# Eight query tiles regrouped over three attention rounds of a two-layer adaLN transformer kernel

## The reference, cut to what matters

```python
# h = layernorm(x) * (1 + ca) + sa              [4, 1024, 256]
latent_kv = h @ w_kv_down                       # rank 128
k, v = split(latent_kv @ w_kv_up)               # 16 heads of 64 each
q = h @ w_q                                     # 16 heads of 64
att = einsum('bqhd,bkhd->bhqk', q, k) * 64**-0.5
att = softmax(where(causal, att, -inf), axis=-1)
y = einsum('bhqk,bkhd->bqhd', att, v).reshape(B, T, 1024)
x = x + ga * (y @ w_out)
```

## Time and profile before

| What | Value |
|---|---|
| median of 3 runs | 1795.16 us |
| profiled execution, its span | 1797.59 us, 1796.3 us |
| TensorE busy | 1737.0 us, 97% |
| VectorE busy | 1250.7 us, 70% |
| ScalarE busy | 887.7 us, 49% |
| GpSimd busy | 854.0 us, 48% |
| granted TensorE clock, mean | 0.999 of full |
| one pair in the steady part of the attention (second batch) | 25.07 us |

### The profile page before, as it was taken

One profiled execution on the slowest core, in us unless ns is written; L12 is line 12 of the kernel. 1 busy time (PEld: TensorE's weight loads), 2 busy tenths in 40 slices (PEclk: granted clock), 3 DMA queues, 4 the chain that ended last, 5 costly groups with the idle time before them and its releaser, 6 DMA issues.

```text
span 1796.3 us, 40559 instructions
## 1 busy us (share of the span) xinstructions
PE 1737.0 (97%) x16006; PEld 1207.7 (67%) x16006; DVE 1250.7 (70%) x2766; ACT 887.7 (49%) x1968; POOL 854.0 (48%) x1282
## 2 busy tenths in 40 slices
PE   9999999999999999999999999999999999999998
PEld 5666685668566767566856667756685666766667
DVE  5888848626788885753678887675468888676545
ACT  4676634223577763322457775432246767443233
POOL 2777842221187874241138777314114877731410
PEclk9999999999999999999999999999999999999999
DMA  6555570321255554040135555305013555530500
GB/s 185 129 134 127 125 208 31 54 42 37 69 138 128 128 120 149 1 81 15 37 92 131 130 126 122 133 2 95 0 43 103 134 126 124 132 109 2 94 1 25
DMA packets 119915, 164.42 MB, mean 92 GB/s; under 512 B 30032, under 2 KB 86832, under 8 KB 118704
## 3 DMA queue, kind: packets, MB, share of 16 engines
q1 hardware_dynamic: 105760, 155.03, 35.9%
q10 hardware_dynamic: 13968, 6.82, 1.3%
HBM read 63.16 MB, written 4.24 MB: 38 GB/s over the span
## 4 chain that ended last, share of the span: by engine, by line
PE 72%; DVE 14%; ACT 5%; SPq 4%; DMA 3%; issue 1%; POOL 1%; ACTq 0%; DVEq 0%; POOLq 0%
PE scores L466 13%; PE bank L684 10%; PE scores L664 9%; PE bank L719 4%; PE bank L466 4%; SPq L1002 4%; DVE prob L813 3%; ACT prob L924 2%; PE scores L1776 2%; PE scores L1686 2%; PE scores L1114 2%; DMA placed<-prob 2%; PE bank L725 2%; PE bank L721 2%; PE scores L1748 2%; PE scores L437 2%
## 5 line engine op out<-in xcount | busy, mean ns | idle before, releaser
L882 POOL COPY placed<-prob 32x768 f32<-32x768 f32 x384 | 315.5, 822 | 27.5
L297 POOL TENSOR_TENSOR rstd<-rstd,minus_half 128x2 f32<-128x2 f32 x96 | 69.7, 728 | 533.1 <-DVE rstd L296 531.0
L684 PEld LDWEIGHTS bank<-placed,v_t 128*64 128x64 f32 x4608 | 250.0, 137 | 75.7 <-issue 70.5
L684 PE MATMUL bank<-placed,v_t 128*64 128x128 f32 x4608 | 272.7, 275 | 9.9 <-DMA placed<-hx 4.8
L664 PE MATMUL scores<-k_t,q_t 64*128 64x512 f32 (+3 forms) x1536 | 275.1, 496 | 0.8 <-ACT rec_t L934 0.8
L806 DVE CUSTOM_DVE_ANT_0 mod_rows<-scores,hx 128x128 f32<-128x128 f32 (+7 forms) x256 | 191.8, 749 | 75.5 <-PE scores L664 75.5
L813 DVE STREAM_TRANSPOSE prob<-prob 128x1536 f32<-128x1536 f32 x128 | 222.9, 1765 | 27.4 <-ACT prob L924 27.1
L806 DVE CUSTOM_DVE_ANT_0 x<-scores,hx 128x128 f32<-128x128 f32 (+7 forms) x256 | 192.7, 753 | 0.0
L924 ACT ACTIVATE prob<-mod_rows,neg_max 128x128 f32<-128x128 f32 (+2 forms) x192 | 137.3, 715 | 102.9 <-DVE neg_max L806 86.6
L664 PEld LDWEIGHTS scores<-k_t,q_t 64*128 64x128 f32 x1536 | 129.5, 186 | 85.1 <-issue 62.0
L870 POOL COPY rec_wide<-rec 128x128 f32<-128x128 f32 x256 | 65.0, 289 | 226.6 <-DVE rec L817 168.6
(11 more groups left out here) (249 smaller groups left out, 3435.8 us busy)
## 6 DMA issues: line engine op xcount, KB each, us to landing
placed<-prob SPq DMA_DIRECT2D x640, 96.0 KB, 2.2
f<-in_L_ffn_f SPq DMA_DIRECT2D x16, 2048.0 KB, 13.6
placed<-hx SPq DMA_DIRECT2D x320, 96.0 KB, 2.2
mod_rows<-mod_scratch SPq DMA_DIRECT2D x32, 128.0 KB, 4.3
out<-x SPq DMA_DIRECT2D x16, 256.0 KB, 2.2
w_ring<-in_L_attn_w_q ACTq DMA_DIRECT2D x24, 128.0 KB, 2.6
w_ring<-in_L_attn_w_kv_up ACTq DMA_DIRECT2D x48, 64.0 KB, 2.0
next_x<-in_L_attn_x SPq DMA_DIRECT2D x6, 512.0 KB, 4.1
```

The costliest lines, as they stand in the source:

```text
L297: step = pool.do(lambda e, ts=ts: nc.gpsimd.tensor_tensor(rstd[:, ts], rstd[:, ts], minus_half[:, ts], op=ALU.pow), var, filled)
L684: last = nc.tensor.matmul(out_bank[rows_, at_:at_ + P], v_t[pair % 2][:, j, rows_], placed[m % 2][:, :, head, first_block(m, i) + j, :], s ...
L882: nc.gpsimd.tensor_copy(placed[m % 2][target * GROUP:(target + 1) * GROUP, source, :, :, :], prob[m % 3][source * GROUP:(source + 1) * GRO ...
```

## The change

Which tiles share a round, and in which order they are worked on, changes. No instruction is of another shape, and there are as many of each shape as before. A round still has 12 blocks. A has the tiles 3, 5, 1 (6 parts), B has 7, 2, 0 (6 parts), C has 4, 6 as before (4 parts). `out_parts` follows: the three tiles 1, 3, 5 of A are evenly spaced and are copied and normalised by one instruction in place of two. Those of B (0, 2, 7) need two in place of one.

```diff
-        ROUND_TILES = ((0, 2, 1, 5), (3, 7), (4, 6))
+        ROUND_TILES = ((3, 5, 1), (7, 2, 0), (4, 6))
@@
         def out_parts(m):
-            return [(0, 2)] if len(tiles_in(m)) == 2 else [(0, 3), (3, 4)]
+            return [(0, 2), (2, 3)] if 7 in tiles_in(m) else [(0, len(tiles_in(m)))]
```

## The result

The changed kernel took 1847.57 us in the median of 4 runs (1846.05 to 1851.0), the kernel before 1794.65 us (4 runs, one more than in the table above). The ratio is 1.0297, with a 95% interval of 1.0279 to 1.0315: slower by 53 us. The profiled execution has a span of 1846.2 us, 49.9 more than before; the one of the kernel before was 2.9 us above its median, so what follows accounts for 50 of the 53. In the experiments the kernel before was timed again beside each group of runs, with medians of 1795.1 to 1795.5 us, so times of different sections can be compared to within about 1 us.

A forecast was written before the change was run, and what follows sets the result against it. TensorE's own order was taken to bound the steady rounds. B's waits 27.4, moves 8.8 and first rounds 13.2 gave +49.4 on 1797.6, 1847.0 profiled; with the median 2.4 lower, 1845 was forecast, range 1822 to 1868.

The forecast's parts named there:

- TensorE bound, nothing removed: Steady rounds: TensorE's own order sets the time; the change removes none of its work, nought in sum.
- The wait before k1: Each steady round B with projections: k1 waits 1.14 us for ScalarE's copy, bounds 0.9 to 1.4; 27.4 us in all.
- The steps 2.03, 3.30, 7.19, 7.60: Round B, us after scores begin: first minimum starts, its exponential starts, five exponentials end, copy ends and k1 starts.
- The wait for k1 covers the late shuffles: Rounds B and C: shuffles end later, but C's minima start just on time, so the two delays are not added.
- The moves of B: SyncE's ten DMAs after B's shuffles: values wait longer in 24 rounds, 7 x 0.77 + 17 x 0.2 = 8.8 us; bounds 0, 31.
- Rounds 0 to 3: First rounds, VectorE and ScalarE chain: +0.6 in round 0, +1.9 in 1, +0.8 in 3; 3.3 per batch, 13.2 us together.
- Tail: Last pair and output projections: nothing waits for the late copy and the projections keep their order; nought.
- The rival with slow moves: Moves of B at their upper bound, every last move taking 4.1 us: +72 us, 1867; chance 0.15.
- The rival by which the copy is not in the way: Round B: k1's wait is met earlier; only first rounds and some moves stay, +13 to +22, about 1812; chance 0.10.
- the one by which small last parts let the shuffles start sooner: Rounds A and B: small last part saves 0.76 us each, move waits go, first rounds shorten by 9; 1783; chance 0.04.
- "same" and "faster": Whole kernel's outcome: same, within 0.2% or 3.6 us, chance 0.04; faster, chance 0.05; slower had 0.91.
- no change: Rival for the whole kernel: everything hides behind TensorE, added exponentials use only slack; 1795; chance 0.05.

## Why the prediction was right, and where it was off

1845 was forecast, 1847.6 measured. The mechanism in the steady rounds is the one described, step for step; two terms of the sum were mis-sized, in opposite directions.

- **TensorE bound, nothing removed**: held. Counts are equal, and the kernel with the largest tile last takes the time of before.
- **The wait before k1**: forecast 1.14 us in each of 24 rounds, measured 1.05. The steps 2.03, 3.30, 7.19, 7.60 came out as 2.02, 3.37, 7.23 (the start of the copy) and 7.73; the semaphore's 0.04 was 0.15. k1 was due at 6.46 by the forecast and at 6.68 (7.73 - 1.05) in the trace. When TensorE has to stop in the middle of the block, the two pieces of L721 take 1.12 + 1.10 us in place of 1.98, 0.24 more. This term was missing. With it and the transposes (B one fewer, C one more) B and C together lost 1.29 us per pair, 31.0 in all, not 27.4. The 0.24 us, 24 times, is also 5.8 of the 12.4 us by which TensorE's busy time grew, where the prediction had it near 1737.
- **"The wait for k1 covers the late shuffles"**: held, and it is the step that the run with B's copy early shows. The prediction put that C would keep most of the delay; C kept 0.8 us of wait and the moves took the rest (7.7 us more, 0.3 in each A).
- **The moves of B**: mis-sized. Forecast 8.8 us more, measured nought (3.3 before and after). The time that the moves have fell from 9.5 to 8.9 us (621.41 - 612.47; 8.7 forecast), but 17 of 24 rounds still had no wait: ten issues take 6.2 to 7.5 us in this run, and most often what was left sufficed. The 0.77 and 0.2 us were my choice, and both were too large; the sign "waits of the values for moves of B grow" did not show. At 7.4 us to give, in the run with all copies early, all 24 wait.
- **Rounds 0 to 3**: mis-sized the other way. Forecast 13.2, measured 19.7. The chain of VectorE and ScalarE was priced rightly: with the clock held in three batches, 13.8 remain, and in each of these the minima of round 2 start 2.5 us later than before (19.0 against 16.5, forecast 0.6 + 1.9) and rounds 0 to 3 take 3.1 to 3.2 us more (forecast 3.3). What failed is not in the sum at all: it took TensorE's durations at full clock after a wait that the new order made 4.0 us long. That was worth the other 5.9.
- **Tail**: forecast nought, measured -1.4. In the last pair TensorE waited 3.8 us for the moves of C in place of 4.8; where the rest comes from stays open.
- The rival with slow moves did not come. The rival by which the copy is not in the way is refuted by the 24 waits, and the one by which small last parts let the shuffles start sooner by the timeline of B above: the last minima were done 1.59 us before the shuffle could start, because ScalarE was still behind. The chances given for "same" and "faster" (0.04 and 0.05) are those of the two rivals changed about (0.05 for no change, 0.04 for faster); nothing else rests on them.

The errors nearly cancel (-8.8 on the moves, +6.5 on the first rounds, +3.6 on the split block, -1.4 at the end), so the closeness of the sum owes something to luck.

## What to carry to other kernels

A queue that one engine works off in order carries other engines' releases with it: before parts are reordered or made smaller, work out how long what stands ahead of each release that a bound engine waits for will take, and when it can start; the number of parts alone says little. A large piece at the head of a round delays its first consumer by a whole bank and puts every fixed cost behind it; here it was better last. And when a wait is found in a trace, compute what is late next before moving it: here the second wait was nearly as long as the first.

## What the runs showed of the hardware that was not expected

In round 1 of the changed kernel, in the second batch, TensorE had no work for 4.00 us. The granted clock fell from 1.00 to 0.50 of full, the lower of its two levels (1.2 in place of 2.4 GHz), while it was idle, and the next 1536 columns of scores took 4.28 us in place of 2.85. After an idle stretch of 2.81 us the clock stayed at 1.00 in all three batches of the run with k0's copy early. In the run with all copies early, the same wait of 2.81 us at nearly the same place was followed by a stretch (496 to 500 us) at 0.60 in the mean:

```profile
496.00:500.00 4.00, 3.81 (x15) 2.62 (x17) 2.23 (x2) 3.44 (x12) 2.15 (x3) 0.60 0.65 151
```

The Trainium skill (TensorE: Matmul & The Clock Gate, "What's actually happening") says that the gate is set by how busy TensorE has been recently. The runs agree with that, and they show that the same wait can go either way: of nine waits of 2.81 us at the same place in three kernels (the second to fourth batch of each), five left the clock at 1.00 and four were followed by a fall, one of these in a kernel where the other two waits left it alone.
